# Cross-attention of a decoder block: operands padded to 128 rows and columns, the squares of the exponentials on GpSimd

## The chip, the core and the metric

The kernel runs on one core of a Trainium2 chip (trn2). The metric is the device time of one execution in microseconds. TensorE multiplies, VectorE (DVE), ScalarE (ACT) and GpSimd (POOL) work on rows, SyncE (SP) issues the transfers.

## What is computed

One decoder layer on 64 sequences of 128 rows of 128 features: causal self-attention with 16 heads of 8, cross-attention to a context of 77 rows, and a feed-forward part with 8 low-rank experts of which 2 are used. The change is in cross-attention:

```python
qk = jnp.einsum('bhqd,bhkd->bhqk', Q, K)
scores = qk / math.sqrt(dk)
mean_sim = scores.mean(axis=(-2, -1))
max_sim = scores.max(axis=-1).mean(axis=-1)
probs = jax.nn.softmax(scores, axis=-1)
entropy_proxy = jnp.var(probs, axis=-1, ddof=1).mean(axis=-1)
feats = jnp.stack([mean_sim, max_sim, entropy_proxy], axis=-1)
...
t = jnp.exp(log_t)[..., None]
attn = jax.nn.softmax(qk / (2.0 * t), axis=-1)
out = jnp.einsum('bhqk,bhkd->bhqd', attn, V)
```

The temperature `t` of each batch and head comes from a small network on three features: mean score, mean of the row maxima, and variance of the softmax. So the scores are needed twice: once query by key for the features, and once key by query, scaled by 1/(2t), for the output. The variance needs the sum of the exponentials and the sum of their squares.

## The kernel before

Three stages follow each other: `self_attention`, `cross_attention`, `expert_ffn`, with a small normalisation step before each. The order of the work in each stage is written by hand: every engine has its own list of calls, one pass over steps `n`, and semaphores tie them.

In `cross_attention` a step n handles batch n in its first half (features) and batch n - 11 (`LAG`) in its second half (output), since temperatures are worked out for groups of 8 batches. Steps 11 to 63 have both halves; the last eleven have only the second.

First half, batch n. `scores_outer` and `scores_inner` (L1037, L1048) form the scores of 16 heads in PSUM tile SQ. To keep accuracy each operand is split in a high and a low part, so each product is made three times (high x high, high x low, low x high). Heads are separated by masks: of 32 rows (one quad of four heads) a masked copy KMH, KML is made by GpSimd (`key_masks`), and a product uses 32 rows, so that products of several quads can run side by side in different row strips of TensorE. VectorE takes the row maxima (`row_max`, L881), TensorE transposes them (`max_transpose`), ScalarE copies them negated into mT (`mT_copy`), TensorE subtracts them inside SQ (`subtract_max`, L1060: mT has 16 rows, `heads` is a matrix of ones and zeros), ScalarE takes exponentials into E1 (`exp_e`, L766), VectorE sums them (`sum_e`), ScalarE squares them into E2 (`square`, L776), VectorE sums those (`sum_e2`). SQ is one tile: the scores of the next batch wait for `exp_e`.

Second half, batch b = n - 11, in two halves h = 0 and 1 of 8 heads (`by_key`, L1067). Into PSUM tile SK (77 of 128 rows used) come first two shift products (minus the scaled maximum of each query, brought by four small transfers into rows 0, 32, 64, 96 of `shift`; 1 row of ones as the other operand), then 3 x 2 products of 32 rows with the 77 keys as columns. ScalarE takes the exponentials into P (`exps`), and `pv` (L1082) multiplies P with the values VA, four products of 32 columns side by side. Transposes, a division (`norm`), the output projection and the residual follow.

## Time and profile before

| | |
|---|---|
| three runs | 2082.62, 2084.21, 2085.64 us; median 2084.21 |
| profiled execution | 2087.13 us, its span 2085.3 us |
| mean granted TensorE clock | 0.765 |
| busy share of the span | TensorE 91%, VectorE 62%, ScalarE 45%, GpSimd 32% |
| cross-attention | from about 555 us to 1418 us |

A granted clock of 1.00 is 2.4 GHz, 0.50 is 1.2 GHz. "Busy" is time in which the engine has an instruction on record; products on TensorE overlap, so a busy TensorE is not at its peak. A name like L1074 is a line of the kernel; xa_ marks tiles of cross-attention, sa_ of self-attention, ff_ and fh_, fl_ of the experts.

### The profile page before, as it was taken

The numbers are of one execution on the slowest core, as the hardware profiler recorded it, in microseconds if no ns is written. First come the engines' busy times: TensorE is split into PE (matmuls) and PEld (weight loads), VectorE is DVE, ScalarE is ACT, GpSimd is POOL, SyncE is SP. The second block draws the span as 40 slices with busy tenths as digits, with TensorE's granted clock in tenths as the row PEclk, the third lists the DMA queues.
The fourth block names the chain that finished last, engine by engine and source line by source line (L and its number), as shares of the span: only waits on it lengthen the run. The fifth ranks groups of instructions, "written<-read, shape, count | busy, mean of one in ns | idle before, by whom it ended". The sixth has DMA issues, their size and how long they took to land. (4 is left out here: it accounts for less than half of the span.)

```text
span 2085.3 us, 42401 instructions
## 1 busy us (share of the span) xinstructions
PE 1907.7 (91%) x14484; PEld 1419.8 (68%) x14484; DVE 1287.3 (62%) x2961; ACT 943.2 (45%) x2047; POOL 672.6 (32%) x746
## 2 busy tenths in 40 slices
PE   1999999999678999999999999995898988989888
PEld 0555555555355766676666766544898988989888
DVE  4666666666456555555555555315777777777775
ACT  1455545555345555555655565433333333333332
POOL 1344333444223333333332333221233232332322
PEclk9999999999755555555555555556999999999998
DMA  5000000000000000000000000000000000000000
GB/s 143 2 2 1 1 1 1 1 1 1 6 6 4 6 5 5 5 5 6 5 5 5 6 5 2 2 2 1 6 8 5 8 7 5 8 5 8 8 5 11
DMA packets 26229, 16.50 MB, mean 8 GB/s; under 512 B 6098, under 2 KB 23444, under 8 KB 26132
## 3 DMA queue, kind: packets, MB, share of 16 engines
q1 hardware_dynamic: 26132, 15.23, 2.7%
q8 instruction: 58, 0.95, 0.2%
q14 instruction: 39, 0.32, 0.1%
HBM read 9.97 MB, written 4.19 MB: 7 GB/s over the span
## 5 line engine op out<-in xcount | busy, mean ns | idle before, releaser
L794 ACT ACTIVATE xa_P<-xa_SK 77x1024 f32<-77x1024 f32 x128 | 130.6, 1020 | 161.0 <-PE xa_SK L1078 161.0
L280 ACT ACTIVATE sa_P<-sa_SK 128x1024 f32<-128x1024 f32 x128 | 131.2, 1025 | 149.8 <-PE sa_SK L423 149.8
L1397 ACT ACTIVATE ff_SG<-bank 128x512 f32<-128x512 f32 x128 | 76.7, 599 | 266.7 <-PE bank L1614 266.7
L353 DVE TENSOR_REDUCE sa_mx<-sa_SQ 128x8 f32<-128x1024 f32 x128 | 156.5, 1223 | 10.2 <-PE sa_SQ L423 8.7
L246 POOL TENSOR_TENSOR sa_KM<-sa_HQK,sc_headmask 128x512 fp32r<-128x512 f32 x64 | 66.6, 1041 | 297.1 <-ACT sa_HQK L275 297.1
L1519 DVE TENSOR_TENSOR ff_GU<-ff_SG,bank 128x512 f32<-128x512 f32 x128 | 87.3, 682 | 111.3 <-ACT ff_SG L1397 111.3
L1679 PE MATMUL bank<-fh_r,ff_GH 128*128 128x256 f32 x512 | 154.9, 303 | 0.0
L1612 PE MATMUL bank<-ff_ZH,fh_b 128*128 128x256 f32 x512 | 154.0, 301 | 0.0
L1614 PE MATMUL bank<-ff_ZH,fl_b 128*128 128x256 f32 x512 | 152.9, 299 | 0.0
L1613 PE MATMUL bank<-ff_ZL,fh_b 128*128 128x256 f32 x512 | 152.2, 297 | 0.0
L1680 PE MATMUL bank<-fl_r,ff_GH 128*128 128x256 f32 x512 | 152.1, 297 | 0.0
L1681 PE MATMUL bank<-fh_r,ff_GL 128*128 128x256 f32 x512 | 151.9, 297 | 0.0
L727 POOL TENSOR_TENSOR xa_QMH<-xa_QBH,xc_headmask 128x512 fp32r<-128x512 f32 x64 | 72.2, 1128 | 237.0 <-ACT xa_QBH L786 237.0
L1348 POOL TENSOR_TENSOR ff_zz<-ff_zt 128x256 f32<-128x256 f32 x32 | 23.2, 726 | 382.4 <-DVE ff_zt L1535 382.4
L886 DVE TENSOR_REDUCE xa_FEAT<-xa_SQ 128x12 f32<-128x924 f32 x64 | 71.7, 1121 | 118.6 <-PE xa_SQ L1033 118.6
L1092 PE MATMUL xa_O<-xa_P,xa_VA 77*32 77x128 f32 x2048 | 138.3, 421 | 0.0
L1525 DVE TENSOR_TENSOR ff_GL<-ff_GU,ff_GH 128x512 fp32r<-128x512 f32 x128 | 130.8, 1022 | 0.0
L712 POOL TENSOR_TENSOR xa_LK<-xa_QK,xa_HK 128x77 fp32r<-128x77 f32 x64 | 22.5, 352 | 330.0 <-DVE xa_HQ L879 330.0
L893 DVE TENSOR_REDUCE xa_ZS<-xa_E 128x16 f32<-128x1232 f32 x64 | 91.8, 1434 | 59.7 <-ACT xa_E L773 59.0
L1033 PE MATMUL xa_SQ<-xa_KMH,xa_HQ 32*128 32x308 f32 (+1 forms) x320 | 105.9, 528 | 13.6 <-ACT xa_E L773 13.6
L1356 POOL TENSOR_TENSOR ff_ZH<-ff_AH,ff_M 128x512 fp32r<-128x512 f32 x64 | 83.0, 1296 | 98.0 <-ACT ff_M L1387 98.0
L1679 PEld LDWEIGHTS bank<-fh_r,ff_GH 128*128 128x128 f32 x512 | 107.9, 211 | 0.0
(248 smaller groups left out, 5970.5 us busy)
## 6 DMA issues: line engine op xcount, KB each, us to landing
xa_shift<-xa_row SPq DMA_DIRECT2D x256, 2.0 KB
out<-X SPq DMA_DIRECT2D x64, 64.0 KB, 1.5
xa_cx<-ctx SPq DMA_DIRECT2D x64, 38.5 KB
sa_shift<-sa_mT SPq DMA_DIRECT2D x64, 8.0 KB, 1.8
fr_b<-L_ffn_B SPq DMA_DIRECT2D x2, 256.0 KB, 4.0
fr_r<-down_a SPq DMA_DIRECT2D x1, 512.0 KB, 4.9
fr_w<-L_ffn_w_gate SPq DMA_DIRECT2D x1, 256.0 KB, 3.5
fr_w<-L_ffn_w_up SPq DMA_DIRECT2D x1, 256.0 KB, 3.7
```

What stands on the lines that cost most here:

```text
L280: nc.scalar.activation(P[:, 2 * (k % 2) + h, :], SK[:], ACT.Exp).then_inc(p_ready, 1)
L353: nc.vector.tensor_reduce(mx[:, p, 2 * JH * h:2 * JH * h + 2 * JH], SQ[:].rearrange("q (j k) -> q j k", k=T), AX.X, ALU.max).then_inc(max_ ...
L794: nc.scalar.activation(P[:, (2 * b + h) % 4, :], SK[0:TC, :], ACT.Exp).then_inc(p_ready, 1)
L1033: return mm(SQ[:, at:at + n * TC], queries[rows, b % QRING], keys[rows, b % 2, j:j + n].rearrange("c j k -> c (j k)"), start=start, stop=stop,
L1092: last = mm(O[32 * t:32 * t + 32, h * T:h * T + T], VA[:, b % VRING].rearrange("k e x -> k (e x)")[:, 256 * e + 32 * u:256 * e + 32 * u + 32],
L1525: nc.vector.tensor_tensor(GG[1][:, k % 4, :], GU[:, k % 2, :], GG[0][:, k % 4, :].bitcast(F32), ALU.subtract).then_inc(gl_done, 1)
L1612: mm(out, w[0], x[0], start=start, stop=False, **kw)
L1613: mm(out, w[0], x[1], start=False, stop=False, **kw)
L1614: return mm(out, w[1], x[0], start=False, stop=stop, **kw)
L1679: mm(out, h, RD[0][:, f, :], start=(s == 0 and f == 0), stop=False, skip_group_check=True)
L1680: mm(out, h, RD[1][:, f, :], start=False, stop=False, skip_group_check=True)
L1681: last = mm(out, l, RD[0][:, f, :], start=False, stop=(s == 1 and f == 3), skip_group_check=True)
```

## The change

It does five things. HK, LK (the keys' parts), mT, VA, P, `heads` and `shift` are used with 128 rows or columns, the added part filled with zeros once by GpSimd at the stage's start. SK gets 128 rows. The shift product reads all 128 rows of `shift` against `pick`, whose rows 0, 32, 64 or 96 are ones. `subtract_max` reads 128 rows. The square moves from ScalarE to GpSimd, as a product of E1 with itself, behind the query masks. TensorE, ScalarE, VectorE and the transfers' queue now wait for all of the setup (`SETS` from 3 to 8). The diff, cut where hunks only narrow an index to the used part (`[0:TC]`, `[0:H]`):

```diff
@@ -553,8 +553,8 @@
         bias = sb("bias", [1, C])
-        ones = sb("ones", [128, TC], F32R)
-        heads = sb("heads", [H, H * TC], F32R)
+        pick = sb("pick", [128, QUADS, T], F32R)
+        heads = sb("heads", [128, H * TC], F32R)
         shift = sb("shift", [128, 2, JH, T], F32R)
...
@@ -563,14 +563,14 @@
         LQ = sb("LQ", [C, QRING, T], F32R)
-        HK = sb("HK", [C, SLOTS, TC], F32R)
-        LK = sb("LK", [C, SLOTS, TC], F32R)
-        VA = sb("VA", [TC, VRING, 2, PART])
+        HK = sb("HK", [C, SLOTS, T], F32R)
+        LK = sb("LK", [C, SLOTS, T], F32R)
+        VA = sb("VA", [128, VRING, 2, PART])
         KMH = sb("KMH", [C, 2, JH, TC], F32R)
         ksum = sb("ksum", [C, SLOTS])
-        mT = sb("mT", [H, SLOTS, T], F32R)
+        mT = sb("mT", [128, SLOTS, T], F32R)
         E1 = sb("E1", [128, 2, H * TC])
...
@@ -591,7 +591,7 @@
         row = sb("row", [H, T], F32R)
-        P = sb("P", [TC, 4, 2 * JH * T])
+        P = sb("P", [128, 4, 2 * JH * T])
         o = sb("o", [128, 2 * T])
...
@@ -690,6 +690,7 @@
                 load(b)
+            sp.wait_ge(const_set, SETS)
             for n in STEPS:
...
@@ -698,18 +699,29 @@
         def _(pool):
+            nc.gpsimd.memset(ones_row[:], 1.0).then_inc(const_set, 1)
+            nc.gpsimd.memset(shift[:].bitcast(F32), 0.0).then_inc(const_set, 1)
+            nc.gpsimd.memset(HK[:].bitcast(F32), 0.0).then_inc(const_set, 1)
+            nc.gpsimd.memset(LK[:].bitcast(F32), 0.0).then_inc(const_set, 1)
+            nc.gpsimd.memset(mT[:].bitcast(F32), 0.0).then_inc(const_set, 1)
             nc.gpsimd.memset(VA[:], 0.0).then_inc(const_set, 1)
-            pool.wait_ge(const_set, 1)
-            units = VA[:, :, :, 0:32 * (H // 2)].rearrange("k s e (u x) -> k (s e) u x", x=32)
+            pool.wait_ge(const_set, 6)
+            units = VA[0:TC, :, :, 0:32 * (H // 2)].rearrange("k s e (u x) -> k (s e) u x", x=32)
             nc.gpsimd.memset(units[:, :, :, DK:DK + 1], 1.0).then_inc(const_set, 1)
-            nc.gpsimd.memset(ones_row[:], 1.0).then_inc(const_set, 1)
+            nc.gpsimd.memset(P[:], 0.0).then_inc(const_set, 1)
             pool.wait_ge(loaded, ALL_LOADED)
             by_head = headmask[:].unsqueeze(2)
+
+            def square(b):
+                pool.wait_ge(e1_ready, b + 1)
+                need(pool, z2_done, b)
+                nc.gpsimd.tensor_tensor(E2[:], E1[:, b % 2], E1[:, b % 2], ALU.mult).then_inc(e2_ready, 1)
 
                 s, q = slot(b), b % QRING
-                nc.gpsimd.tensor_tensor(LK[:, s], QK[:, s, T:T + TC], HK[:, s].bitcast(F32), ALU.subtract).then_inc(l_ready, 1)
+                nc.gpsimd.tensor_tensor(LK[:, s, 0:TC], QK[:, s, T:T + TC], HK[:, s, 0:TC].bitcast(F32),
+                                        ALU.subtract).then_inc(l_ready, 1)
                 nc.gpsimd.tensor_tensor(LQ[:, q], QK[:, s, 0:T], HQ[:, q].bitcast(F32), ALU.subtract).then_inc(l_ready, 1)
...
@@ -734,6 +746,8 @@
                     query_masks(n - LAG + 1)
+                if real(n - 1):
+                    square(n - 1)
                 if real(n + 2) and not late:
...
@@ -772,11 +786,6 @@
                                      scale=1.0 / R8).then_inc(e1_ready, 1)
-
-            def square(b):
-                act.wait_ge(e1_ready, b + 1)
-                need(act, z2_done, b)
-                nc.scalar.activation(E2[:], E1[:, b % 2], ACT.Square).then_inc(e2_ready, 1)
 
...
@@ -817,9 +826,11 @@
             act.wait_ge(loaded, ALL_LOADED)
-            nc.scalar.activation(ones[:], ident[:, 0:TC], ACT.Copy, bias=1.0, scale=0.0).then_inc(act_set, 1)
+            rows4 = ident[:].rearrange("k (g r) -> k g r", r=32)[:, :, 0:1]
+            nc.scalar.copy(pick[:], rows4.to_broadcast([128, QUADS, T])).then_inc(act_set, 1)
             nc.scalar.copy(heads[:].rearrange("h (g k) -> h g k", k=TC),
-                           ident[0:H, 0:H].unsqueeze(2).to_broadcast([H, H, TC])).then_inc(act_set, 1)
+                           ident[:, 0:H].unsqueeze(2).to_broadcast([128, H, TC])).then_inc(act_set, 1)
+            act.wait_ge(const_set, SETS)
             act.wait_ge(bias_ps, 1)
...
@@ -835,8 +846,6 @@
                     xcT_copy(n + 2)
-                if real(n - 1):
-                    square(n - 1)
                 if real(n - LAG - 1):
...
@@ -859,6 +868,7 @@
             dve.wait_ge(loaded, ALL_LOADED)
+            dve.wait_ge(const_set, SETS)
             for f, scale in enumerate((1.0 / (T * TC * R8), 1.0 / (T * R8), 1.0 / T)):
...
@@ -1071,11 +1081,11 @@
                 for a, _, r in quads:
-                    mm(bank(SK, a)[0:TC], ones[r:r + 1], shift[r:r + 1, b % 2].rearrange("c j t -> c (j t)"),
+                    mm(bank(SK, a), pick[:, r // 32], shift[:, b % 2].rearrange("c j t -> c (j t)"),
                        start=True, stop=False)
                     for a, rows, _ in quads:
-                        last = mm(bank(SK, a)[0:TC], keys[rows, slot(b)],
+                        last = mm(bank(SK, a), keys[rows, slot(b)],
                                   queries[rows, b % 2].rearrange("c j t -> c (j t)"), start=False, stop=(part == 2))
```

`heads[:, ...]` and `mT[:, slot(b)]` in `subtract_max`, and VA and P in `pv`, are written without a row range, so the larger tiles alone make these products 128 rows deep.

On GpSimd, one step in the middle of the stage. QMH, QML are the query masks, LK, LQ the low parts of batch n + 2, KMH, KML its key masks. Before:

```order
L727 TENSOR_TENSOR xa_QMH<-xa_QBH,xc_headmask 128x512
L727 TENSOR_TENSOR xa_QML<-xa_QBL,xc_headmask 128x512
L712 TENSOR_TENSOR xa_LK<-xa_QK,xa_HK 128x77
L713 TENSOR_TENSOR xa_LQ<-xa_QK,xa_HQ 128x128
L720 TENSOR_TENSOR xa_KMH<-xa_HK,xc_headmask 128x308
L720 TENSOR_TENSOR xa_KML<-xa_LK,xc_headmask 128x308
```

and changed:

```order
L739 TENSOR_TENSOR xa_QMH<-xa_QBH,xc_headmask 128x512
L739 TENSOR_TENSOR xa_QML<-xa_QBL,xc_headmask 128x512
L718 TENSOR_TENSOR xa_E<-xa_E 128x1232
L723 TENSOR_TENSOR xa_LK<-xa_QK,xa_HK 128x77
L725 TENSOR_TENSOR xa_LQ<-xa_QK,xa_HQ 128x128
L732 TENSOR_TENSOR xa_KMH<-xa_HK,xc_headmask 128x308
L732 TENSOR_TENSOR xa_KML<-xa_LK,xc_headmask 128x308
```

The square has come in behind the query masks and ahead of the four instructions for batch n + 2.

On TensorE, the second half of a step, from the transpose of the maxima (the letters x2, x8 count equal rows; the last two numbers are output rows and columns). Before:

```order
L1058 MATMUL xa_O<-xc_ident,xa_FEAT 16x128
L1074 MATMUL xa_SK<-xa_shift,xa_ones 77x512 x2
L1078 MATMUL xa_SK<-xa_QMH,xa_HK 77x512 x2
L1078 MATMUL xa_SK<-xa_QML,xa_HK 77x512 x2
L1078 MATMUL xa_SK<-xa_QMH,xa_LK 77x512 x2
L1063 MATMUL xa_SQ<-xa_heads,xa_mT 128x462 x2
L1063 MATMUL xa_SQ<-xa_heads,xa_mT 128x308
```

and changed:

```order
L1068 MATMUL xa_O<-xc_ident,xa_FEAT 16x128
L1084 MATMUL xa_SK<-xa_shift,xa_pick 128x512 x2
L1088 MATMUL xa_SK<-xa_QMH,xa_HK 128x512 x2
L1088 MATMUL xa_SK<-xa_QML,xa_HK 128x512 x2
L1088 MATMUL xa_SK<-xa_QMH,xa_LK 128x512 x2
L1073 MATMUL xa_SQ<-xa_heads,xa_mT 128x462 x2
L1073 MATMUL xa_SQ<-xa_heads,xa_mT 128x308
```

The order is the same; the shapes have grown.

## Rows read from the trace of the kernel before

**Rows 1.** The page, parts 1 and 2: busy time, and the granted clock in 40 slices.
```profile
PE 1907.7 (91%) x14484; PEld 1419.8 (68%) x14484; DVE 1287.3 (62%) x2961; ACT 943.2 (45%) x2047; POOL 672.6 (32%) x746
...
PEclk9999999999755555555555555556999999999998
```

**Rows 2.** Busy time by stretch: us, then PE, PEld, DVE, ACT, POOL busy, granted clock, DMA.
```profile
100.00:300.00 200.00, 200.00 (x1869) 118.11 (x1858) 137.35 (x316) 102.33 (x212) 80.41 (x80) 1.00 0.01 1
...
800.00:900.00 100.00, 99.56 (x686) 68.79 (x678) 54.01 (x109) 58.12 (x137) 34.70 (x49) 0.50 0.02 5
...
1440.00:1445.00 5.00, 4.67 (x22) 4.67 (x23) 1.03 (x1) 1.96 (x3) 2.91 (x3) 0.50 0.00 0
...
1445.00:1450.00 5.00, 5.00 (x42) 5.00 (x42) 2.97 (x10) 1.39 (x3) 0.00 (x0) 0.96 0.00 0
...
1485.00:1490.00 5.00, 3.17 (x29) 2.96 (x28) 4.28 (x16) 2.18 (x6) 0.73 (x1) 0.98 0.00 0
...
1490.00:1495.00 5.00, 5.00 (x33) 5.00 (x32) 4.96 (x8) 2.17 (x5) 4.09 (x3) 0.68 0.00 0
```

**Rows 3.** Groups by line, 800 to 1200 us: shapes, count, busy us, mean ns.
```profile
L1074 PE MATMUL xa_SK<-xa_shift,xa_ones 1*77 1x512 f32 x130 | 46.0, 705 | 0.0
...
L794 ACT ACTIVATE xa_P<-xa_SK 77x1024 f32<-77x1024 f32 x65 | 66.3, 1020 | 61.4 <-PE xa_SK L1078 61.4
...
L779 ACT ACTIVATE xa_E<-xa_E 128x1232 f32<-128x1232 f32 x33 | 40.6, 1230 | 0.0
```

**Rows 4.** Timeline of one step, 896.60 to 908.42: start, us, engine, line, operation.
```profile
896.60 0.62 PE L1033 MATMUL xa_SQ<-xa_KMH,xa_HQ 32*128 32x308 f32 x2
...
901.26 1.12 DVE L886 TENSOR_REDUCE xa_FEAT<-xa_SQ 128x12 f32<-128x924 f32 x1 [2.11 <-PE xa_SQ L1033]
...
903.11 0.66 PE L1102 MATMUL xa_R<-xc_ident,xa_o 128*128 128x128 f32 x2
...
903.91 0.71 PE L1074 MATMUL xa_SK<-xa_shift,xa_ones 1*77 1x512 f32 x2
...
904.34 0.75 PE L1063 MATMUL xa_SQ<-xa_heads,xa_mT 16*128 16x462 f32 x1
...
904.42 0.62 PE L1078 MATMUL xa_SK<-xa_QMH,xa_HK 32*77 32x512 f32 x2
...
904.85 0.62 PE L1078 MATMUL xa_SK<-xa_QML,xa_HK 32*77 32x512 f32 x2
...
905.95 1.02 ACT L794 ACTIVATE xa_P<-xa_SK 77x1024 f32<-77x1024 f32 x1 [0.86 <-PE xa_SK L1078]
...
908.42 0.62 PE L1033 MATMUL xa_SQ<-xa_KMH,xa_HQ 32*128 32x308 f32 x2
```

**Rows 5.** Timeline of self-attention, shift and last key product at the upper clock.
```profile
204.40 0.81 PE L442 MATMUL sa_SK<-sa_shift,sa_pick_row 128*128 128x512 f32 x2
...
205.71 0.39 PE L423 MATMUL sa_SK<-sa_QMH,sa_LQK 32*128 32x512 f32 x2
```

**Rows 6.** Timeline of ScalarE in the last steps: the first exponential of two steps.
```profile
1351.31 1.02 ACT L794 ACTIVATE xa_P<-xa_SK 77x1024 f32<-77x1024 f32 x1 [2.16 <-PE xa_SK L1078]
...
1360.14 1.02 ACT L794 ACTIVATE xa_P<-xa_SK 77x1024 f32<-77x1024 f32 x1 [2.16 <-PE xa_SK L1078]
```

**Rows 7.** Timeline of the stage's start, GpSimd and VectorE.
```profile
555.44 6.72 POOL L701 MEMSET xa_VA<- 77x7950 f32 x1 [28.50 <-POOLq L71]
...
555.48 6.80 DVE L863 TENSOR_SCALAR xa_w1s<-xc_w1b 128x64 f32<-128x64 f32 x3 [0.52 <-PEq L71]
```

**Rows 8.** Groups by line, 800 to 1200 us, GpSimd and VectorE.
```profile
L713 POOL TENSOR_TENSOR xa_LQ<-xa_QK,xa_HQ 128x128 fp32r<-128x128 f32 x32 | 13.9, 433 | 0.0
...
L727 POOL TENSOR_TENSOR xa_QML<-xa_QBL,xc_headmask 128x512 fp32r<-128x512 f32 x33 | 34.1, 1035 | 0.0
...
L893 DVE TENSOR_REDUCE xa_ZS<-xa_E 128x16 f32<-128x1232 f32 x32 | 45.9, 1434 | 31.8 <-ACT xa_E L773 31.8
...
L947 DVE SCALAR_TENSOR_TENSOR xa_QBL<-xa_QK,xa_cfc,xa_QBH 128x128 fp32r<-128x128 f32 x33 | 11.6, 351 | 30.5 <-ACT xa_QBH L786 30.5
```

More of the change, by code:

```diff
@@ L650, in cross_attention @@
         ALL_LOADED = 16 * len(CROSS_CONSTANTS)
-        SETS = 3
+        SETS = 8
         PREPARED = 6
@@ L719, in key_masks @@
                         pool.wait_ge(l_ready, 2 * b + 1)
-                    nc.gpsimd.tensor_tensor(tile[:, b % 2], keys[:, slot(b)].unsqueeze(1).to_broadcast([C, JH, TC]),
+                    nc.gpsimd.tensor_tensor(tile[:, b % 2], keys[:, slot(b), 0:TC].unsqueeze(1).to_broadcast([C, JH, TC]),
                                             by_head.to_broadcast([C, JH, TC]), ALU.mult).then_inc(km_ready, 1)
@@ L758, in qkv_copy @@
                 v = M[0:TC, T + TC:2 * T + TC].rearrange("k (u e d) -> k e u d", e=2, d=DK)
-                units = VA[:, b % VRING, :, 0:32 * (H // 2)].rearrange("k e (u x) -> k e u x", x=32)
+                units = VA[0:TC, b % VRING, :, 0:32 * (H // 2)].rearrange("k e (u x) -> k e u x", x=32)
                 nc.scalar.copy(units[:, :, :, 0:DK], v).then_inc(v_sb, 1)
@@ L763, in mT_copy @@
                 act.wait_ge(mT_ps, b + 1)
-                nc.scalar.activation(mT[:, slot(b)], O[0:H, 2 * T:3 * T], ACT.Copy, scale=-1.0).then_inc(mT_sb, 1)
+                nc.scalar.activation(mT[0:H, slot(b)], O[0:H, 2 * T:3 * T], ACT.Copy, scale=-1.0).then_inc(mT_sb, 1)
             def exp_e(b):
@@ L788, in scaled @@
                     act.wait_ge(m_row[(b - 1) % 2], 64 * ((b - 1) // 2 + 1))
-                nc.scalar.activation(row[:], mT[:, s].bitcast(F32), ACT.Copy, scale=cfh[:, s:s + 1]).then_inc(row_sb, 1)
+                nc.scalar.activation(row[:], mT[0:H, s].bitcast(F32), ACT.Copy, scale=cfh[:, s:s + 1]).then_inc(row_sb, 1)
             def exps(b, h):
@@ L793, in exps @@
                 need(act, pv_ps, 2 * b + h - 3)
-                nc.scalar.activation(P[:, (2 * b + h) % 4, :], SK[0:TC, :], ACT.Exp).then_inc(p_ready, 1)
+                nc.scalar.activation(P[0:TC, (2 * b + h) % 4, :], SK[0:TC, :], ACT.Exp).then_inc(p_ready, 1)
             def o_copy(b):
@@ L876, in cast @@
                 need(dve, sk_ps, 2 * (b - SLOTS) + 2)
-                nc.vector.tensor_copy(HK[:, slot(b)], QK[:, slot(b), T:T + TC]).then_inc(h_ready, 1)
+                nc.vector.tensor_copy(HK[:, slot(b), 0:TC], QK[:, slot(b), T:T + TC]).then_inc(h_ready, 1)
                 need(dve, sq_ps, b - QRING + 1)
```

## Prediction

> **What bounds the kernel now.** I read three views in this order. First the page: the 40 slices of granted TensorE clock show 9 (full) for self-attention, 5 from slice 12 to slice 27, and 9 for the experts, while TensorE is 91% busy over the span [rows 1]. So the middle of the kernel, cross-attention, runs at the lower clock. Second, the busy time by stretch [rows 2]: in 800 to 900 us TensorE has 99.56 of 100 us with a product on record, at a granted clock of 0.50 (1.2 GHz). Self-attention in 100 to 300 us is busy all the time too, but at 1.00 (2.4 GHz). ScalarE has 58 us, VectorE 54 us and GpSimd 35 us of the 100, so none of them bounds the stage; TensorE at half clock does. What separates the two stages is the shape of the products: self-attention's shift product fills 128 rows and 128 columns [rows 5], cross-attention's has 1 row and 77 columns [rows 3]. Third, the timeline of one step [rows 4], from one scores product to the same product of the next batch: 896.60 to 908.42, **11.82 us**. Between 800 and 1200 us there are 65 exponential passes, two a step, so a mean step is 400/32.5 = 12.3 us; the 0.5 us above 11.82 is what the eight-batch temperature round adds.
>
> **The sum is made against the profiled execution** (2087.1 us), which is 2.9 us above the median of the three runs; I take the 2.9 off at the end.
>
> **Setup.** The change fills HK, LK, mT, shift and P with zeros on GpSimd, 3 x 2048 + 1024 + 4096 = 11264 elements a partition, and TensorE, ScalarE, VectorE and the DMA queue now wait for all of it. The present memset takes 6.72 us for 7950 elements [rows 7], so the new ones take 11264 x 6.72/7950 = 9.5 us, in front of the first product and covered by nothing. VectorE's first instruction took 6.80 us beside that memset [rows 7], so its few preparations were held anyway; after the wait they come in the open, some 0.5 us. **+10 us.** The Trainium skill says the same of such a pair (SBUF — State Buffer: an instruction in VectorE's two-port mode and a GpSimd instruction block each other fully); the trace agrees with that row. The new `pick` copy on ScalarE is hidden under the memsets.
>
> **Widening at the lower clock.** A column takes its time whatever the number of rows, so padding a product by itself costs nothing: one 512-column pass is 904.85 - 904.42 = 0.43 us [rows 4]. What costs is lost company. The two 1-row shift products lie in different row strips and run side by side: both together took 0.71 us, and one alone 705 ns [rows 3, 4]. With 128 rows they go one after the other, +0.43 us, twice a step: **+0.85**. The maximum's product (16 rows, in the first strip) starts at 904.34, before the key products of the upper strips at 904.42, and is over when they are [rows 4]. With 128 rows it must wait for them: 462 + 462 + 308 = 1232 columns, 1232/512 x 0.43 = **+1.03**; the lower end is 0, should it still fit a gap. The key products keep their 32 rows and their pairs, P and VA keep four column strips, so they cost the same. Lower-clock step: 11.82 + 0.85 + 1.03 = 13.7 us, with the round 14.2. Fifty-three steps have both halves (scores and by-key products, n = 11 to 63): 53 x 1.9 = +101 us. The last eleven have only the by-key half, 1360.14 - 1351.31 = 8.83 us each [rows 6], and get +0.85: +9. The steps before n = 11 have no shift products, and their maximum's product stands alone already: 0. Sum if the clock stays at 0.50: 2087 + 10 + 101 + 9 = **2207 us**.
>
> **The same step at the upper clock.** Follow the ring in [rows 4]. Scores, P times V, transposes, inner scores: 4.66 us (896.60 to 901.26), all TensorE, half of it and 0.1 us of latency: 2.4. Row maximum and residual: 1.85 to 903.11, VectorE, unchanged. Transposes to 903.91: 0.8, halved to 0.4. Shift and key products up to the exponential: self-attention's same piece at the upper clock goes from 204.40 to 205.71 + 0.39 = 1.70 [rows 5]. Exponential, copy, `exp_e`, next scores: 905.95 to 908.42 = 2.47, ScalarE, unchanged. Sum 8.8 us; I take 9.0, because VectorE's copies now meet more GpSimd work. With the round 9.4. So 53 x (12.3 - 9.4) = -154 us. A tail step is two rounds of products and exponential, 2 x (1.70 + 1.02 + 0.1) = 5.7, plus what TensorE does in between; 7.0 is my choice between 5.7 and 8.83, 11 x 1.8 = -20. Sum if the upper clock holds throughout: 2087 + 10 - 154 - 20 = **1923 us**.
>
> **Squares on GpSimd.** One pass of 128 x 1232. Rows of GpSimd: 128 elements 433 ns, 512 elements 1035 ns [rows 8], slope 1.57 ns, so 0.433 + 1104 x 0.00157 = 2.2 us. With no start-up it would be 1232 x 1.57 ns = 1.9, at the 512-element row's whole rate (2.02 ns an element) 2.5: the bounds. GpSimd is 35 us busy in 100 now [rows 2], 4.1 us a step; with 2.2 it is 6.3, under either step. Behind the square in its queue stand `low` and `key_masks` of batch n + 2, which TensorE wants one step later; before it stand the query masks, wanted at the next step's start. ScalarE loses 1.23 us a step [rows 3], which it spent in a gap: 0 us. The closed ring is square, casts and sum_e2, sum_e, QBL, QML, next square: 2.2 + 0.4 + 1.43 + 1.43 + 0.35 + 1.03 and some waits, about 7.5 us [rows 8] (the casts, two instructions, an estimate from QBL's row), shorter than 9.0. **0 us**, and 0.6 us a step at the upper clock if the square takes 3 us.
>
> **Which clock?** That decides, and the trace shows both sides. For the rise: expert stage, 1440 to 1445 at 0.50 with products of 128 rows and columns back to back, then 0.96 [rows 2]. Against holding it: 1485 to 1490, TensorE has only 3.17 of 5 us on record, and the next 5 us are granted 0.68, though every product there is full [rows 2]. The new step has one long full stretch: maximum's product 1.03, a transpose 0.2, P times V 0.85, the next shift pair 0.85, some 3.3 us with gaps. The other 10 us are mostly 32-row products. Once the clock is up, TensorE's work in the 1.85 us of row maximum (project and QKV, 1.95 us now) shrinks to about 1 us, so it idles there each step, next to the narrow inner scores. I read this as bursts: the clock rises in some steps and is lost within one to three. I take the upper clock for a quarter of the way between the two sums: 2207 - 0.25 x 284 = 2136, less 2.9: **2133 us**.
>
> The Trainium skill (TensorE: Matmul & The Clock Gate, Part 1) says that the clock follows how busy the engine has been. By that alone the padding changes no clock, and the result is the first sum; the rows go against it, since 99.56 us busy of 100 stood at 0.50.
>
> **Rivals.** (A) Bursts, as above, the upper clock for 5 to 40% of the way: 2195 to 2095. Chance 0.41. (B) The clock stays down: 2207 - 2.9 = 2204. For it: the full stretch is short, and no slice of this stage stands above 5 now [rows 1]. Against: the expert stage rose soon after full products began. Chance 0.24. (C) The upper clock holds nearly throughout, as in self-attention, whose step also has narrow products beside padded ones: 1923 to 1995. It wins if one wait of about 1 us in each step is not enough to lose the clock. For it: self-attention kept 1.00 although it has narrow score products. Against: its TensorE never waits, and here it would. Chance 0.18. (D) It holds for more than half: about 2050, faster. It is decided at 2207 - 284u = 2087, u = 0.42. Chance 0.17. (E) The padding works but the squares bind: GpSimd's pass, or VectorE held behind it, adds 53 x 0.6 = 32 us to C or D. It is inside their range.
>
> **Numbers.** About 0.2% is what a measurement of this kernel can tell from no change. Faster: C, D less its edge: 0.33. Within 0.2% (2080 to 2088) only a narrow strip of u: 0.04. Slower: A, B and the edge: 0.63. Signs on both sides hold much of the chance; the likeliest case alone, A, is 2095 to 2195. The range leaves out the better half of C, and what lies above B: 1985 to 2208.
>
> **What would show it.** Right: granted clock in the stage between 0.5 and 0.7 in the slices, in bursts; a lower-clock step of 13.7 us and an upper one near 9; the two shift products one after the other (0.85 us at the lower clock); the maximum's product after the key products; first product of the stage 10 us later; squares of 2.2 us on GpSimd with ScalarE's gap wider. Wrong: a clock of 0.9 or more through the stage (C), or lower-clock steps below 13 us (the widened products still find company), or QBL and casts of over 1 us in VectorE's rows with the row maximum late (E).

## The result and the profile after

The changed kernel takes **2008.51 us** (median of four runs, 1995.96 to 2015.18), the kernel before 2083.41 us (four runs beside it). The ratio is **0.9633**, with a 95% interval of 0.9584 to 0.9682: faster by 3.7%, where 2133 us and slower had been forecast. The time lies inside the range (1985 to 2208), on the other side of no change. The profiled execution took 2006.53 us, its span 2004.7, at a mean granted clock of 0.878 where before had 0.765. Below, a run more than 1.5% above the fastest of its kernel (one of e4's, one of e11's, two of e15's) counts in the median but not in the ratio.

The page of the kernel after, busy time and granted clock in 40 slices (the counterpart of [rows 1]):

```profile
PE 1767.6 (88%) x14422; PEld 1320.7 (66%) x14484; DVE 1294.2 (65%) x2961; ACT 867.9 (43%) x1983; POOL 822.2 (41%) x815
...
PEclk9999999999955689897887986558999999999999
```

From slice 15 to slice 24, where before showed 5 after 5, stand 7, 8 and 9. TensorE is less busy (88% against 91%), because its products are over sooner. Busy time by stretch, columns as in [rows 2]:

```profile
580.00:680.00 100.00, 77.10 (x323) 55.28 (x323) 60.54 (x91) 36.00 (x110) 49.26 (x59) 0.50 0.02 5
...
700.00:1200.00 500.00, 454.48 (x4034) 308.54 (x4034) 332.97 (x657) 288.94 (x760) 311.99 (x342) 0.88 0.02 6
...
1250.00:1350.00 100.00, 84.29 (x486) 46.73 (x484) 20.26 (x65) 30.70 (x59) 14.97 (x14) 0.50 0.00 1
```

The steps with scores alone (580 to 680) stay at 0.50, and so does the tail, the last eleven steps (1250 to 1350). Between them the clock is granted to 0.88, while TensorE is busy 454 of 500 us; before it was busy 99.56 of 100 us at 0.50 [rows 2].

The timeline of one regular step of the kernel after, as [rows 4]: first exponential to first exponential, 770.25 to 779.15.

```profile
770.25 1.02 ACT L803 ACTIVATE xa_P<-xa_SK 77x1024 f32<-77x1024 f32 x1 [0.70 <-PE xa_SK L1088]
...
774.24 0.41 PE L1112 MATMUL xa_R<-xc_ident,xa_o 128*128 128x128 f32 x2 [0.84 <-DVE X L975]
...
774.51 0.70 PE L1084 MATMUL xa_SK<-xa_shift,xa_pick 128*128 128x512 f32 x2
...
776.04 0.83 PE L1073 MATMUL xa_SQ<-xa_heads,xa_mT 128*128 128x462 f32 x3
...
779.15 1.02 ACT L803 ACTIVATE xa_P<-xa_SK 77x1024 f32<-77x1024 f32 x1 [0.68 <-PE xa_SK L1088]
```

**8.90 us**, where the lower clock took 11.82. The only wait of TensorE in it is 0.84 us, ahead of the output's transposes, for VectorE's row maximum and residual. The clock does not hold all the time; this is where it falls (timeline of TensorE, then stretches around the first of the two waits):

```profile
822.89 0.41 PE L1112 MATMUL xa_R<-xc_ident,xa_o 128*128 128x128 f32 x2 [1.42 <-DVE X L975]
...
835.53 0.66 PE L1112 MATMUL xa_R<-xc_ident,xa_o 128*128 128x128 f32 x2 [1.24 <-DVE X L975]
```

```profile
822.00:825.00 3.00, 2.11 (x13) 1.33 (x13) 2.63 (x8) 1.53 (x2) 3.00 (x3) 1.00 0.06 16
...
825.00:828.00 3.00, 3.00 (x22) 2.10 (x22) 1.96 (x3) 1.56 (x4) 0.23 (x1) 0.51 0.02 5
...
828.00:832.00 4.00, 4.00 (x51) 2.28 (x39) 1.04 (x6) 3.24 (x11) 0.00 (x0) 0.94 0.01 2
```

In the two steps of each temperature round the same wait is 1.42 and 1.24 us long. The clock falls within some 2 us of it (here at 825.1 and 835.3) and comes back 3 to 20 us later; such a step takes 12 to 15 us. Regular steps with 0.84 us keep the clock up to six times in a row, but in four of the seven stretches between the rounds one of them loses it too, just behind this wait (801.2 to 808.0, a step of 11.9 us).

The timeline of the stage's start on GpSimd, of its first product, and of two steps of the tail on ScalarE:

```profile
551.84 0.19 POOL L702 MEMSET xa_ones_row<- 1x128 f32 x1 [27.79 <-POOLq L71]
...
558.12 6.71 POOL L707 MEMSET xa_VA<- 128x7950 f32 x1
...
565.26 3.56 POOL L711 MEMSET xa_P<- 128x4096 f32 x1
...
568.88 0.59 PE L1143 MATMUL xa_R<-xc_wo,xc_bv 128*1 128x128 f32 x2 [21.94 <-POOL xa_P L711]
...
1295.23 1.02 ACT L803 ACTIVATE xa_P<-xa_SK 77x1024 f32<-77x1024 f32 x1 [2.98 <-PE xa_SK L1088]
...
1305.39 1.02 ACT L803 ACTIVATE xa_P<-xa_SK 77x1024 f32<-77x1024 f32 x1 [2.98 <-PE xa_SK L1088]
```

The squares among the groups by line, 800 to 1200 us (count, busy us, mean ns):

```profile
L718 POOL TENSOR_TENSOR xa_E<-xa_E 128x1232 f32<-128x1232 f32 x39 | 87.2, 2235 | 0.0
```

Where the 80.6 us between the two profiled spans lie follows from three marks on ScalarE, the exponentials of batches 0, 53 and 63. Before they started at 667.91, 1313.37 and 1404.37, after at 676.49, 1222.18 and 1325.73. So up to the first +8.6, the 53 full steps -99.8 (12.18 us each before, 10.30 after), the last ten steps +12.6, and behind them -2.0.

### The profile page after: what moved, and what is told of

It is laid out like the page before. It is cut to its first block and busy times, and to the rows that moved or that the text cites. A ratio compares the mean times of both kernels' runs of the same rounds, so it can differ in the third digit from the quotient of the medians.

```text
span 2004.7 us, 42347 instructions
## 1 busy us (share of the span) xinstructions
PE 1767.6 (88%) x14422; PEld 1320.7 (66%) x14484; DVE 1294.2 (65%) x2961; ACT 867.9 (43%) x1983; POOL 822.2 (41%) x815
## 5 line engine op out<-in xcount | busy, mean ns | idle before, releaser
L718 POOL TENSOR_TENSOR xa_E<-xa_E 128x1232 f32<-128x1232 f32 x64 | 143.1, 2235 | 0.2 <-ACT xa_E L787 0.2
L1084 PE MATMUL xa_SK<-xa_shift,xa_pick 128*128 128x512 f32 x256 | 116.5, 544 | 0.0
L1690 PEld LDWEIGHTS bank<-fl_r,ff_GH 128*128 128x128 f32 x512 | 106.5, 208 | 0.0
L1691 PEld LDWEIGHTS bank<-fh_r,ff_GL 128*128 128x128 f32 x512 | 105.4, 206 | 0.0
```

The source lines that it names most:

```text
L718: nc.gpsimd.tensor_tensor(E2[:], E1[:, b % 2], E1[:, b % 2], ALU.mult).then_inc(e2_ready, 1)
L1690: mm(out, h, RD[1][:, f, :], start=False, stop=False, skip_group_check=True)
L1691: last = mm(out, l, RD[0][:, f, :], start=False, stop=(s == 1 and f == 3), skip_group_check=True)
```

## The experiments

Each kernel was run beside the kernel before on the same chip (medians 2081 to 2085 us). "Clock" is the granted clock of the stage between 700 and 1100 or 1200 us in its profile.

**Theory 1:** the time comes from the clock, and the padding raised it. **Theory 2:** it comes from ScalarE, relieved of the squares.

### e1_squares_alone and e2_padding_alone: the two halves of the change

e1 is the kernel before with the move of the squares:

```diff
-                nc.scalar.activation(E2[:], E1[:, b % 2], ACT.Square).then_inc(e2_ready, 1)
+                nc.gpsimd.tensor_tensor(E2[:], E1[:, b % 2], E1[:, b % 2], ALU.mult).then_inc(e2_ready, 1)
```

e2 is the changed kernel with this line the other way round.

> The kernel before with the squares moved to GpSimd and no padding. Theory 1 (the 75 us come from the granted clock, which the padding raises): the stage stays at 0.50, TensorE bounds it, 2080 to 2088 us, no difference from before. Theory 2 (the gain comes from ScalarE's shorter queue, the clock only follows): about 2010 to 2050 us.

> The changed kernel with the squares back on ScalarE, in their old place. Theory 1: the clock is up for most of the stage as in the changed kernel (0.83 to 0.95 a 100 us), 2005 to 2030 us; the 1.23 us pass may delay an upper-clock step of 8.9 us by 0 to 0.5 us. Theory 2: nothing of the gain is left, 2084 us or more, up to the 2204 us of the recorded low-clock sum.

Measured: e1 2086.91 us, ratio 1.0015 (1.0005 to 1.0024); e2 2011.84 us, ratio 0.9657 (0.9641 to 0.9673). Their stretches, e1 first:

```profile
700.00:1100.00 400.00, 398.26 (x2711) 276.20 (x2712) 215.81 (x435) 196.52 (x507) 208.17 (x228) 0.50 0.02 5
```

```profile
700.00:1200.00 500.00, 455.01 (x4090) 310.29 (x4090) 324.75 (x658) 345.70 (x811) 205.89 (x294) 0.89 0.02 6
```

Theory 2 falls. The squares on GpSimd alone bring nothing (3 us slower, if anything), though ScalarE has 49 us of 100 to do instead of 58 [rows 2]. The padding alone brings the clock (0.89) and the whole gain; the changed kernel's 0.9633 and e2's 0.9657 have overlapping intervals.

### e3_shift_one_row, e4_max_16_rows, e5_keys_77: which padding

The changed kernel with one part narrow again. e3, and then e4:

```diff
-                    mm(bank(SK, a), pick[:, r // 32], shift[:, b % 2]...
+                    mm(bank(SK, a), pick[r:r + 1, r // 32], shift[r:r + 1, b % 2]...
```

```diff
-                    ... mT[:, slot(b)], heads[:, 6 * a * TC:(6 * a + n) * TC],
+                    ... mT[0:H, slot(b)], heads[0:H, 6 * a * TC:(6 * a + n) * TC],
```

e5, its first line of five; the others do the same to the shift products' output and weights, and to the rows of VA and P:

```diff
-                        last = mm(bank(SK, a), keys[rows, slot(b)],
+                        last = mm(bank(SK, a)[0:TC], keys[rows, slot(b), 0:TC],
```

> The changed kernel with the shift products back to one row of weights and of shifts (still 128 output columns). Theory 1a (the shift pair, 2 x 512 columns twice a step, carries the clock): the stage falls back to 0.50; 2087 + 10 (setup) + 55 (maximum's product alone, 53 x 1.03) = about 2150 us. Theory 1b (the maximum's product or the wider P times V and key products carry it): clock as in the changed kernel, pair of shift products side by side again, 1990 to 2010 us.

> The changed kernel with the maximum's product back to its 16 rows. Theory 1a (the shift products carry the clock): clock as in the changed kernel, 1985 to 2010 us, the product in a gap again. Theory 1b (the maximum's product, 1232 columns in a row, carries it): 0.50 through the stage, 2087 + 10 + 54 (shift pairs, 64 x 0.85) = about 2150 us. If each full stretch counts, something between, 2030 to 2120 us.

> The changed kernel with keys, exponentials and values back to 77 (the by-key products and the shift products write 77 columns, P times V contracts over 77 rows); the 128 rows of the shift and maximum's products stay. Theory 1a (the shift products' 128 rows carry the clock alone): 2000 to 2025 us as the changed kernel. Theory 1c (the 128 columns are needed as well): the stage falls back to 0.50 for the most part, 2130 to 2204 us.

Measured: e3 2144.06 us, ratio 1.0325 (1.0264 to 1.0386); e4 2021.67, 0.9674 (0.9631 to 0.9716); e5 2086.77, 1.0031 (0.9999 to 1.0063). The stage in e3, e4 (the profiled execution is the longest of its four, 2048 us) and e5:

```profile
700.00:1100.00 400.00, 393.26 (x2578) 274.47 (x2582) 207.73 (x419) 190.17 (x484) 197.89 (x217) 0.55 0.02 5
```

```profile
700.00:1200.00 500.00, 461.90 (x3805) 303.11 (x3798) 307.02 (x615) 272.42 (x714) 289.60 (x318) 0.75 0.02 6
```

```profile
700.00:1100.00 400.00, 376.97 (x2919) 239.83 (x2919) 236.55 (x471) 209.03 (x545) 224.41 (x246) 0.74 0.02 5
```

Without the shift pair's 128 rows the clock is lost almost wholly. The time is near the expected one (2144 for 2150), but two errors cancel there: a lower-clock step takes 13.11 us, where 11.82 + 1.03 = 12.85 was expected, some 14 us more over the stage, and some 20 us come back where the clock is up, mostly in one burst of three steps of 8.3 to 8.5 us. Without the maximum's rows the clock is lost in part: 0.75 in this profile, and over the whole kernel 0.838 to 0.863 in the four runs against 0.875 to 0.883 in the changed kernel's. In time the two ratios' intervals overlap. With 77 columns, too, it is lost in part, and the whole gain with it: 128 rows are not enough. Of the three, each is needed for the changed kernel's clock; the shift pair weighs most.

### e7_tail_one_row and e8_pads_later: the two places that got slower

e7 takes one row for the shift products of the last eleven batches; e8 fills the zeros of the keys' last columns, `shift` and P on GpSimd in steps 1 to 6.

```diff
+                    k = slice(0, 128) if b < B - LAG else slice(r, r + 1)
+                    mm(bank(SK, a), pick[k, r // 32], shift[k, b % 2]...
```

```diff
-            nc.gpsimd.memset(HK[:].bitcast(F32), 0.0).then_inc(const_set, 1)
...
+            pads = {1: [HK[:, :, TC:T].bitcast(F32), LK[:, :, TC:T].bitcast(F32)], 2: [shift[:].bitcast(F32)],
+                    3: [P[:, 0]], 4: [P[:, 1]], 5: [P[:, 2]], 6: [P[:, 3]]}
```

> The changed kernel with the shift products of the last eleven batches (no scores beside them) on one row again. Their steps ran at 0.50 and took 10.17 us against 8.83 before. Theory: the shift pairs are side by side again, step 8.8 us, 11 x 1.3 = 14 us off, about 1995 us; the experts' start is not changed. Rival: the full products of the tail bring the clock up earlier for the experts, so that half of it is given back, about 2002 us.

> The changed kernel with the zeros of the keys' last 51 columns, of shift and of P filled in steps 1 to 6 of the stage, and mT's before step 0. Theory (the fill stands alone in front of the first product): first product of the stage 9 to 10 us earlier, 1999 us. Rival: VectorE is held while GpSimd fills, and the steps that get a fill grow by as much; then 2003 to 2009 us.

Measured: e7 2001.00 us, ratio 0.9594 (0.9568 to 0.9621); e8 2003.48, 0.9603 (0.9569 to 0.9637). Both lie below the changed kernel's 2008.51, by less than its runs spread (1996 to 2015), so that the totals settle neither. The traces do. A tail step is 9.01 us in e7 against 10.17. In e8 the second exponential over batch 0's scores ends 25.7 us after GpSimd's first instruction of the stage, in the changed kernel 34.6 us: 9 us, as expected. e8's profile shows as well what the changed kernel's hardly has, a step with both halves wholly at the lower clock, here the second such step (ScalarE's timeline, then the stretch; below it the same step before the change):

```profile
678.54 1.02 ACT L805 ACTIVATE xa_P<-xa_SK 77x1024 f32<-77x1024 f32 x1 [2.48 <-PE xa_SK L1094]
...
692.18 1.02 ACT L805 ACTIVATE xa_P<-xa_SK 77x1024 f32<-77x1024 f32 x1 [2.32 <-PE xa_SK L1094]
```

```profile
678.50:692.20 13.70, 13.70 (x83) 9.24 (x79) 5.78 (x10) 5.73 (x16) 6.42 (x7) 0.50 0.02 5
```

```profile
677.79:688.99 11.20, 11.20 (x83) 7.91 (x79) 5.86 (x11) 6.71 (x17) 4.21 (x6) 0.50 0.03 6
```

13.64 us looks like the 13.7 of the prediction, but this step has no output projection yet, and before the change it took 11.20 us and not 11.82. So the padding costs 2.44 us a step at the lower clock, where 1.88 had been forecast, and a regular step would take 11.82 + 2.44 = 14.3 us (an estimate: the traces of the changed kernel and of e8 have none wholly at 0.50). A step near the end of e2 gives the same: 13.74 us against 11.29 before.

### e9_fill_3 and e15_fill_one_row: is it the wait?

Three products whose result nobody reads, in the wait ahead of the output's transposes, in each step with both halves:

```diff
+            def fill(b, count):
+                pe.wait_ge(p_ready, 2 * b + 1)
+                for i in range(count):
+                    mm(bank(SK, i % 2), pick[:, 0], heads[:, 0:512], start=True, stop=True)
...
+                if real(n) and real(n - LAG):
+                    fill(n - LAG, 3)
```

e15 has the same three with one row of `pick` and `heads` each.

> The changed kernel with three products of 128 rows and 512 columns, whose result nobody reads, in TensorE's wait ahead of the output's transposes in each step with both halves (idle 0.84 us in a regular step, 1.2 to 1.4 us in the two steps of a temperature round, where the clock falls each time). Theory 3 (the clock is lost over this wait): clock 0.95 or more through the stage, no regular step over 9.0 us, 1940 to 1975 us. Rival (it is lost over the narrow products of those steps): clock as in the changed kernel, and the steps at 0.50 grow by 1.3 us, 2010 to 2025 us.

> The changed kernel with three fill products in the same wait as in e9_fill_3, but of one row of weights each. Theory 4 (the fill acts by being full): no help, clock 0.83 to 0.95 a 100 us as in the changed kernel, 2005 to 2030 us. Rival (the fill acts by covering the wait, whatever its shape): clock 0.97 to 1.00 and 1960 us as with full ones.

Measured: e9 **1959.44 us** (1957.30 to 1961.87), ratio 0.9404 (0.9381 to 0.9427); e15 2034.94 us, the median of 2017.03, 2019.37, 2050.51 and 2069.40, for which there is no ratio. e9's stage, its fill in TensorE's timeline, and e15's stage:

```profile
700.00:1100.00 400.00, 388.38 (x3663) 266.38 (x3662) 294.41 (x575) 251.60 (x665) 274.00 (x300) 0.99 0.03 7
```

```profile
879.07 0.94 PE L1080 MATMUL xa_SK<-xa_heads,xa_pick 128*128 128x512 f32 x3
...
888.77 0.96 PE L1080 MATMUL xa_SK<-xa_heads,xa_pick 128*128 128x512 f32 x3
...
890.20 0.41 PE L1117 MATMUL xa_R<-xc_ident,xa_o 128*128 128x128 f32 x2 [0.47 <-DVE X L975]
```

```profile
700.00:1100.00 400.00, 388.05 (x3274) 256.73 (x3278) 262.86 (x517) 226.83 (x595) 243.63 (x267) 0.86 0.02 6
```

The clock is held at 0.99 and the time is 49 us below the changed kernel's. Work that computes nothing makes the kernel faster, and the step is still 8.9 us: only the losses are gone (steps of a temperature round 10.8 and 10.4 us, not 12 to 15). e15 keeps TensorE as busy (388.05 and 388.38 of 400 us) and stays at 0.86, and its steps at the lower clock pay for the fill. Its three products take 0.73 us, since two of them run side by side, where e9's take 0.94, so they leave a little more of the wait open, and that could be the reason. The waits that are left speak against it. First a step of e15, then one of e9:

```profile
978.04 0.49 PE L1117 MATMUL xa_R<-xc_ident,xa_o 128*128 128x128 f32 x2 [0.18 <-DVE X L975]
...
901.73 0.41 PE L1117 MATMUL xa_R<-xc_ident,xa_o 128*128 128x128 f32 x2 [0.89 <-DVE X L975]
```

e15 loses the clock behind a wait of 0.18 us (1.00 before 978, 0.50 from 978.6 on), and e9 keeps it through one of 0.89 (1.00 from 895 to 910). So covering the wait is not what does it. What acts is that the fill's products are full.

### e10_fill_max_16, e11_fill_shift_1, e14_before_fill: which full products can be spared

The diffs are those shown: e9 with the maximum's product narrow (e4's edit), e9 with the shift products narrow (e3's edit), and the kernel before, all narrow and with ScalarE's squares, with three fill products of the same shape (made from copies of the identity matrix).

> The kernel with the three fill products (e9_fill_3) and the maximum's product back to 16 rows. With the clock held at 1.00 by shift pairs and fill, the maximum's product goes into a gap beside the key products again, and the upper-clock step of 8.9 us gets shorter by up to its 0.5 us: 53 x 0.5 = 27 us, about 1933 us. Rival: without its full stretch the clock falls again (clock 0.65 to 0.81 per 100 us in e4_max_16_rows), 1970 to 2010 us.

> The kernel with the three fill products and the shift products on one row. Theory (what counts is how much of a step TensorE spends in products of full rows and columns, whichever they are): the pair gave four such products a step and the fill gives three, so the clock is up for a part of the stage, 1980 to 2060 us. Rival (fill in the wait is enough by itself): 1.00 throughout and shift products side by side, 1940 to 1960 us. Rival (the shift pair is needed where it is): clock as in e3_shift_one_row, 2150 us and more for the added products, up to 2210 us.

> The kernel before, with nothing widened and the squares on ScalarE, and three full products (128 rows, 128 x 512 columns) that nobody reads in the wait ahead of the output's transposes. Theory 4 (full products raise and hold the clock wherever they stand; widening the kernel's own is one way of having them): the stage at 1.00, steps of 8.4 us, about 1925 us. Rival (the widened shift, maximum's and key products must be there as well): the clock stays at 0.50 and a step gets three products longer, 53 x 1.3 = 69 us: 2153 us.

Measured: e10 1945.82 us, ratio 0.9343 (0.9318 to 0.9368); e11 **1931.33**, 0.9264 (0.9224 to 0.9304); e14 2085.91, 0.9999 (0.9973 to 1.0025). Their stages:

```profile
700.00:1100.00 400.00, 376.36 (x3797) 248.07 (x3797) 303.67 (x594) 259.84 (x687) 281.75 (x308) 1.00 0.03 7
```

```profile
700.00:1100.00 400.00, 385.29 (x3875) 265.30 (x3874) 309.60 (x609) 269.31 (x701) 285.80 (x311) 1.00 0.03 7
```

```profile
700.00:1100.00 400.00, 393.36 (x2807) 276.58 (x2804) 221.94 (x437) 232.13 (x543) 136.10 (x196) 0.59 0.02 5
```

With the fill, either of the two widenings can go. The steps are 8.69 us (e10) and 8.46 us (e11) against 8.91, so at the upper clock the wide maximum's product costs 0.22 us a step and the wide shift pairs 0.45. Even the pair, without which e3 lost the clock, is not needed where it is, though e11 holds the clock less surely: one of its four runs took 1959 us, at 0.888 over the whole kernel where the others have 0.899 to 0.910. Not all of e11's gain is in these steps: of the 35.6 us between the profiled spans of e9 and e11, 19.7 lie in the 53 full steps and 10.7 in the last ten, where the narrow pairs bring the step from 10.17 to 9.01 us. But the fill alone, with nothing widened, does not do it: 0.59, what the clock gives and what the fill costs cancel, and my theory that fill can stand for all of it falls.

### e12_tail_fill, e13_first_fill, e16_before_fill_all, e17_fill_all_pool: the ends of the stage

e12 is e9 with e8's zeros and, in the last eleven steps, two full products into SQ after each half of the by-key products. e13 is e9 with six fill products in steps 0 to 10. e16 is e14 with three in place of e12's two; e17 is e16 with the squares on GpSimd.

```diff
+                if n >= B and real(n - LAG):
+                    fill_tail(2)
```

```diff
+                if real(n) and n < LAG:
+                    for i in range(6):
+                        mm(bank(SK, i % 2), pick[:, 0], heads[:, 0:512], start=True, stop=True)
```

> The kernel with the three fill products, the zeros filled later (as in e8_pads_later), and in the last eleven steps two full products after each half of the by-key products. Theory: the clock is held there too, a step goes from 10.17 us to 7 to 8 us, 11 x 2.7 = 29 us, and 6 us from the zeros: about 1925 us. Rival: the clock stays down in the tail, as the expert stage's waits lose it too; then each step grows by 4 x 0.43 = 1.7 us, 1959 - 6 + 19 = 1972 us.

> The kernel with the three fill products, and six more in the same place in the steps 0 to 10, which have no by-key products and take 8.33 us at 0.50 with TensorE busy 64 of 100 us. Theory: the clock rises there, and with it the halves of the scores and transposes that lie on the ring get shorter: 6.5 to 7.5 us a step, 10 to 20 us off, about 1945 us. Rival: it stays at 0.50; six products are 2.6 us for a wait of 1.9 us, so each step grows by 0.7 us or more, 1967 us.

> e14_before_fill and, in the last eleven steps, three full products after each half of the by-key products. Theory 4: the clock is held in the tail too, a step of 7.2 us there (e12_tail_fill's last five) or less, 11 x 1.8 = 20 us off e14: about 1905 us. Rival: as e12_tail_fill, half of the tail at 0.50 with steps of 12 us, e14's time or some 10 us more.

> e16_before_fill_all with the squares on GpSimd. Theory: ScalarE's 1.23 us pass is off an upper-clock step only where ScalarE is on the ring; between e16's time and 20 us less (53 x 0.4). Rival (it makes no difference, as between e2_padding_alone and the changed kernel): within 5 us of e16.

Measured: e12 1932.49 us, ratio 0.9279 (0.9244 to 0.9315); e13 1971.69, 0.9455 (0.9431 to 0.9478); e16 2118.40, 1.0155 (1.0107 to 1.0204); e17 2123.96, 1.0202 (1.0177 to 1.0228). The tail of e12, and then a step of e16's:

```profile
1180.00:1215.00 35.00, 33.59 (x171) 18.39 (x175) 4.45 (x15) 9.76 (x18) 6.41 (x6) 0.50 0.01 1
...
1215.00:1260.00 45.00, 42.17 (x384) 23.88 (x376) 8.54 (x29) 17.81 (x35) 10.69 (x10) 0.98 0.01 2
```

```profile
1224.91 1.02 ACT L805 ACTIVATE xa_P<-xa_SK 77x1024 f32<-77x1024 f32 x1 [1.73 <-PE xa_SK L1103]
...
1232.11 1.02 ACT L805 ACTIVATE xa_P<-xa_SK 77x1024 f32<-77x1024 f32 x1 [1.73 <-PE xa_SK L1103]
```

```profile
1378.85 1.02 ACT L795 ACTIVATE xa_P<-xa_SK 77x1024 f32<-77x1024 f32 x1 [2.67 <-PE xa_SK L1089]
...
1390.66 1.02 ACT L795 ACTIVATE xa_P<-xa_SK 77x1024 f32<-77x1024 f32 x1 [2.67 <-PE xa_SK L1089]
```

e12's tail comes up half way through; until then its steps take 11.4 to 12.3 us, then 7.2 us instead of 10.17. So the tail's fill is only a part of the gain: of the 28.8 us between the profiled spans of e9 and e12, 15.5 lie ahead of the first exponential, 8.5 in the last ten steps and 4.4 behind them. e16, with narrow shift pairs and more fill, never comes up there and pays 11.81 us a step instead of 8.83 [rows 6]. e13's clock rises for part of the first steps (0.65 in 590 to 650 us, against 0.50), but they take 8.4 to 10.5 us for 8.33: the fill stands ahead of the maximum's transpose and so in the closed chain of work (the ring) that sets the step, and delays it by more than the clock gives. e17 is 6 us above e16, with intervals that overlap: the move of the squares gains nothing here either.

### e18_best and e19_best_max_16: a version that beats both

e18 is e11 with e8's zeros and, in the tail, wide shift products and three full products after each half. e19 also narrows the maximum's product and has a fourth fill product in its place.

```diff
+                    k = slice(r, r + 1) if b < B - LAG else slice(0, 128)
+                    mm(bank(SK, a), pick[k, r // 32], shift[k, b % 2]...
...
+                if n >= B and real(n - LAG):
+                    fill_tail(3)
```

> e11_fill_shift_1 (three full products in the wait, shift products on one row) with the zeros filled later, and for the last eleven steps wide shift products and three full products after each half. Expected: stage at 1.00 with steps of 8.46 us as in e11; the tail's steps 7.2 us as the last five of e12_tail_fill, the clock held from the first of them or back after fewer steps than there: 1931 - 6 (zeros) - 11 x 1.8 = about 1905 us, faster than both kernels. If the tail loses the clock at its start as in e12, about 1920 us.

> e18_best with the maximum's product on 16 rows and a fourth full product in the wait in its place. If full products can stand for each other, the clock is held (1.00) and the step gets 8.46 - 0.2 = 8.25 us (as e10_fill_max_16 against e9_fill_3): 53 x 0.2 = 11 us less than e18. Rival (with neither the shift pair nor the maximum's product wide the clock is lost for part of the stage, as in e14_before_fill, 0.59): 1980 to 2100 us.

Measured: e18 **1899.90 us** (1893.40 to 1902.10), ratio **0.9110** (0.9086 to 0.9135), against the kernel before, and 109 us below the changed one. e19 2015.96, ratio 0.9694 (0.9663 to 0.9725). e18's page, its tail and two of its steps:

```profile
PEclk9999999999975579999999999979999998999999
```

```profile
1160.00:1226.00 66.00, 62.23 (x525) 36.01 (x525) 13.33 (x47) 27.19 (x52) 17.30 (x17) 1.00 0.01 2
```

```profile
1187.74 1.02 ACT L805 ACTIVATE xa_P<-xa_SK 77x1024 f32<-77x1024 f32 x1 [1.87 <-PE xa_SK L1104]
...
1195.40 1.02 ACT L805 ACTIVATE xa_P<-xa_SK 77x1024 f32<-77x1024 f32 x1 [1.88 <-PE xa_SK L1104]
```

and e19's stage:

```profile
700.00:1100.00 400.00, 384.11 (x3226) 274.80 (x3229) 249.95 (x503) 223.42 (x581) 236.18 (x258) 0.76 0.02 6
```

e18's clock is up from the third full step to the end of the tail, with steps of 8.46 and 7.67 us. A fourth fill product did not stand in for the maximum's wide one: e19 goes back and forth between steps of 8.45 us and of up to 14.06 us outside the temperature rounds.

## Why the prediction was wrong

**The failed step** is the one that chose the clock: "I take the upper clock for a quarter of the way between the two sums". On the same scale (2207 to 1923) the profiled execution at 2006.5 stands at 0.71 of the way, and the full steps, 10.30 us between 14.2 and 9.4, at 0.81. The forecast's break-even was at 0.42, so the sign of the change followed from this share. The reading under it was "the clock rises in some steps and is lost within one to three". It took one wait of about 1 us a step for enough to lose it, from a stretch of the expert stage with 1.8 us of nothing on record in 5 [rows 2]. The runs showed that in the changed kernel a wait of 0.84 us a step seldom loses it (up to six regular steps in a row keep it), and that it falls in every temperature round, at waits of 1.2 to 1.4 us. That is rival C's condition met in most regular steps and missed in the two of eight that belong to a round, which gives a time between C and A: D. I had put 0.17 there. The wait was also the wrong thing to judge by on its own: e15 lost the clock behind 0.18 us and e9 kept it through 0.89. Whether the step's products were full or narrow counted as much.

**The evidence for the rise was read too weakly.** I counted one long full stretch of 3.3 us and set the rest aside as 32-row products. e3, e4 and e5 show that the shift pairs, the maximum's product and the 128 columns (with P times V's 128 rows) all add to it.

**The sizes of the terms.** Most were close; the cost of the padding at the lower clock was not.
- Setup, +10: from GpSimd's first instruction to the first product 17.0 us, against 7.5 before (555.44 [rows 7] to 562.89): +9.6.
- Lower-clock step, 13.7: about 14.3, as worked out under e8. The padding costs 2.44 us a step and not 1.88. The narrowed kernels show where the sum was short: e5, with the pairs and the maximum's product wide and 77 columns, has regular steps of 14.01 us, so that these two cost 2.19, not 1.88, and the 128 columns and P times V's 128 rows, put at nothing, about 0.25. By this and the tail's term below, the first sum, 2207, was some 35 us too low, and the share of the way a little larger than above. The changed kernel's time doesn't show it, since it spent few steps there.
- Upper-clock step, 9.0: 8.90, and 9.33 with the rounds in e9, for 9.4. The wide pairs cost half of 0.85 there, 0.45 (e9 less e11).
- Squares, 2.2 us at a cost of 0: 2.235 us, and e1 and e17 find no gain and at most 3 to 6 us of cost; e2 and the changed kernel don't differ by more than their runs spread. Rival E, the squares binding, did not come: QBL takes 350 ns as before [rows 8].
- Tail, +0.85 a step at the lower clock: the clock stayed down, but the step grew from 8.83 to 10.17, +1.33. This term was short by 0.5 us. e7, narrow pairs and wide keys, has 9.01: the keys' 128 columns and P times V's 128 rows cost 0.17 where I had nothing, and the two pairs 1.16. An upper-clock tail step, 7.0 here, was 7.2 in e12, with four fill products in it. So the second sum's tail never came about without fill: e9, up in nearly all full steps, took 1959 us where 1923 had been worked out.
- The ends of rival A, 5 and 40% of the way, are by the two sums 2190 and 2091 us, not 2195 and 2095. Nothing hangs on it.

**Of what would show it wrong**, "a clock of 0.9 or more through the stage" came nearly so (0.88).

The Trainium skill (TensorE: Matmul & The Clock Gate, Part 1) has the clock follow how busy the engine is. By that rule e1, busy 398 of 400 us, would be up, and e10, busy 376, would be the lower; the traces have 0.50 and 1.00. The measurement decides, as it did in the prediction, which then drew too little from it.

**Open.** Which of the padding's rows and columns weigh how much is not settled beyond the order: e4's stage clock rests on one profile, that of the longest of its four runs. The 128 columns of keys were tried only together with P times V's 128 rows. Why a full product counts for more than a narrow one of the same length, no run here shows. e8's 9 us at the stage's start show in the trace and not clearly in the total.

## What to carry to other kernels

Where TensorE bounds a stage and the granted clock says 0.50 although the engine is busy all the time, make the stage's products full before cutting them, and cheap ones first: zeros in unused rows and columns, and full products that nobody reads in waits that are there anyway. Price both sums, the one in which the clock stays and the one in which it rises, and don't guess the share between them from one wait; try it with one kernel for each padding. Here the paddings together were worth 3.5%, the fill without them nothing (e14), and the best choice of both, with the zeros filled later, 9%. Fill that stands on the ring itself, or where the clock stays down, only costs (e13, e16's tail).

## What the runs showed of the hardware that I had not expected

- A wait of 0.84 us in each 8.9 us step left the granted clock at 1.00 for up to six steps in a row; in the temperature rounds, with about 1.4 and 1.25 us, it fell each time.
- The same wait filled by three products of one row: clock 0.86. By three of 128 rows: 0.99. TensorE's busy time was the same (388 of 400 us). e10 was busy for 376 of 400 us only, and had 1.00.
- Zeros did not keep it down: `pick` and `shift` are almost all zeros, and the products with them raised and held the clock.
- A clock that goes up and down spreads the times: the changed kernel's runs lie 1% apart (1996 to 2015 us), those of the kernel before, always down in this stage, 0.2%, and e9's, up in nearly all of it, 0.2% (1957 to 1962). A profile at 1.00 does not promise that: e11's runs lie 1.8% apart.
- Two 1-row shift products side by side save 0.58 us a pair at the lower clock where they stand on the ring alone (e7's tail), not only the 0.43 us of one 512-column pass [rows 4].
